# One product of 512 columns for the high and low parts of a gathered chunk, and a window sum folded by VectorE

## The reference

```python
def _mean_aggregate(x, src, dst, n_nodes):
    msg = x[src]                                              # gather 100,000 rows
    summed = jax.ops.segment_sum(msg, dst, num_segments=n_nodes)
    deg = jax.ops.segment_sum(ones, dst, num_segments=n_nodes)
    return summed / jnp.maximum(deg, 1.0)[:, None]

def _sage_conv(x, src, dst, Wl, bl, Wr, n_nodes):
    return _mean_aggregate(x, src, dst, n_nodes) @ Wl.T + bl + x @ Wr.T

# layer 0: messages weighted by relation and gate, summed over dst, updated, + x, layernorm
x = _layernorm(x + _L0_gnn_ref(x, ...))
# layers 1 to 3: three convolutions, relu behind the first two; then + x, layernorm
h = relu(_sage_conv(x, ..., W1l, b1l, W1r))
h = relu(_sage_conv(h, ..., W2l, b2l, W2r))
x = _layernorm(x + _sage_conv(h, ..., W2l, b2l, W2r))
```

## Time and profile before

| | us |
|---|---|
| median of 3 runs | 3801.09 |
| lowest and highest | 3783.49 and 3802.06 |
| the profiled execution | 3782.04 |
| its span, first to last instruction | 3779.7 |
| PE busy | 3080.2 (81%) |
| DVE busy | 2509.8 (66%) |
| ACT busy | 2338.1 (62%) |
| POOL busy | 2150.0 (57%) |

### The profile page before, as it was taken

One profiled execution on the slowest core, in us unless ns is written; L12 is line 12 of the kernel. 1 busy time (PEld: TensorE's weight loads), 2 busy tenths in 40 slices (PEclk: granted clock), 3 DMA queues, 4 the chain that ended last, 5 costly groups with the idle time before them and its releaser, 6 DMA issues. The chain is left out here.

```text
span 3779.7 us, 55957 instructions
## 1 busy us (share of the span) xinstructions
PE 3080.2 (81%) x17027; PEld 2611.1 (69%) x17027; DVE 2509.8 (66%) x5700; ACT 2338.1 (62%) x4157; POOL 2150.0 (57%) x1993
## 2 busy tenths in 40 slices
PE   5468887887878778777759999949999986999985
PEld 4356666666666666666648888847888865777774
DVE  8857777777777777777736565635555654666676
ACT  1066666666666666666548787728777845777761
POOL 5266666666666666666436555555555555555551
PEclk6589999999998998899979999979999988999998
DMA  4245555555454554455456565455555537555552
GB/s 124 82 128 146 136 138 146 139 135 143 132 141 131 141 136 133 132 140 135 118 188 199 171 192 183 149 175 183 175 178 168 179 107 229 189 175 187 177 155 80
DMA packets 345442, 575.72 MB, mean 152 GB/s; under 512 B 44709, under 2 KB 242678, under 8 KB 345142
## 3 DMA queue, kind: packets, MB, share of 16 engines
q1 hardware_dynamic: 249753, 316.82, 27.2%
q0 software_dynamic: 91872, 252.80, 24.1%
q10 hardware_dynamic: 3517, 2.48, 0.2%
HBM read 487.13 MB, written 84.78 MB: 151 GB/s over the span
## 5 line engine op out<-in xcount | busy, mean ns | idle before, releaser
L1484 POOL DMA_INDIRECT rows_arena<-table_h,src_idx x936 | 989.6, 1057 | 858.4 <-DVE row_pairs L1825 515.9
L1484 POOL DMA_INDIRECT rows_arena<-table_scaled_x,src_idx x782 | 889.4, 1137 | 574.4 <-DVEq L1759 333.4
L2053 PE MATMUL bank<-wide_counts,h_pairs 128*128 128x512 f32 (+1 forms) x4704 | 1085.9, 386 | 155.1 <-ACT wide_counts L1633 125.7
L2053 PEld LDWEIGHTS bank<-wide_counts,h_pairs 128*128 128x128 f32 x4704 | 854.5, 194 | 329.5 <-issue 143.1
L1990 PE MATMUL bank<-rel_pairs,ftype_hot 125*128 125x258 f32 x4688 | 758.0, 312 | 53.0 <-issue 53.0
L1833 DVE TENSOR_TENSOR h_pairs<-rows_arena,h_pairs 128x512 fp32r<-128x512 f32 x600 | 399.5, 681 | 528.7 <-ACT h_pairs L1630 394.4
L1990 PEld LDWEIGHTS bank<-rel_pairs,ftype_hot 125*128 125x128 f32 x4688 | 666.7, 204 | 87.6 <-issue 58.7
L1633 ACT CAST wide_counts<-rows_arena 128x1024 fp32r<-128x1024 bf16 (+1 forms) x600 | 634.7, 1058 | 74.4 <-DMA rows_arena<-edge_counts 74.1
L1630 ACT CAST h_pairs<-rows_arena 128x512 fp32r<-128x512 f32 x600 | 367.7, 613 | 354.8 <-PE bank L2053 213.6
L1654 ACT CAST rows_arena<-bank 128x448 bf16<-128x448 f32 (+1 forms) x940 | 426.4, 505 | 259.1 <-remote 98.8
L2039 PE MATMUL bank<-rows_arena 128*128 128x448 bf16 (+1 forms) x940 | 262.5, 363 | 323.1 <-ACT rows_arena L1654 227.1
(11 more groups left out here) (186 smaller groups left out, 3265.5 us busy)
## 6 DMA issues: line engine op xcount, KB each, us to landing
rows_arena<-edge_counts SPq DMA_DIRECT2D x273, 512.0 KB
edge_counts<-fcount SPq DMA_DIRECT2D x60, 832.0 KB
rows_arena<-in_edge_type_dram SPq DMA_DIRECT2D x195, 187.5 KB
rows_arena<-table_h SPq DMA_DIRECT2D x36, 512.0 KB, 12.1
rows_arena<-table_h,src_idx POOLq DMA_INDIRECT x936
rows_arena<-table_scaled_x,src_idx POOLq DMA_INDIRECT x782
table_h<-chunk_info SPq DMA_DIRECT2D x96, 128.0 KB
rows_arena<-edge_counts SPq DMA_DIRECT2D x39, 256.0 KB
```

The costliest lines, as they stand in the source:

```text
L1484: pool.indirect_dma_start(out=rows[:, g % ring, c, :], out_offset=None, in_=table[:, :], in_offset=bass.IndirectOffsetOnAxis(ap=src_idx[:, ...
L2053: last = pe.matmul(bank[2 + h][:, 0:cols_of(w)], h_pairs[:, v % HALVES, part, b % HALF, h * P:(h + 1) * P], wide_counts[:, v % HALVES, b % ...
```

## The change

The two products of a chunk become one: the moving operand is `row_pairs[slot, :, chunk, :]`, both parts, 512 columns, so the bank holds the sum of the high parts in its first 256 columns and that of the low parts in the other 256. `evacuate` on ACT now copies the second half of the bank to a new tile `window_lo` (one slot for all windows), after a wait for the fold of the window before. A new function on DVE, `fold_window`, adds `window_lo` to the first half of the bank and writes `window_sum`; it signals `s_evac` in ACT's place. It stands in DVE's stream right behind `row_lows(s + 1)`. Layer 0 keeps its code.

```diff
+                    window_lo = sb(f"window_lo{k}", [P, D], F32, tmp)
@@ evacuate, ACT
                                 act.wait_ge(s_seg, last_quad(w) + 1)
+                                if not first:
+                                    if w >= 1:
+                                        act.wait_ge(s_evac, w)
+                                    act.copy(window_lo[:, :], seg_bank[w % 2][:, D:2 * D]).then_inc(s_evac_lo, 1)
+                                    continue
@@ DVE
+                        def fold_window(slot):
+
+                            for w in [w for w in range(windows) if last_quad(w) + 1 == slot]:
+                                dve.wait_ge(s_evac_lo, w + 1)
+                                if w >= 2:
+                                    dve.wait_ge(s_turned, w - 1)
+                                dve.tensor_tensor(window_sum[:, w % 2, 0:D], seg_bank[w % 2][:, 0:D],
+                                                  window_lo[:, :], ALU.add).then_inc(s_evac, 1)
@@ DVE's slot
                                 if s + 1 < groups:
                                     row_lows(s + 1)
+                                fold_window(s)
@@ sums, PE
-                                    for part in range(2):
-                                        last = pe.matmul(seg_bank[w % 2][:, 0:sum_cols], hot[:, g % HOTS, c, :],
-                                                         row_pairs[:, g % ROW_PAIRS, part, c, :],
-                                                         start=(g % GW == 0 and c == 0 and part == 0),
-                                                         stop=(g == last_quad(w) and c == n - 1 and part == 1))
+                                    last = pe.matmul(seg_bank[w % 2][:, 0:2 * D], hot[:, g % HOTS, c, :],
+                                                     row_pairs[:, g % ROW_PAIRS, :, c, :], start=(g % GW == 0 and c == 0),
+                                                     stop=(g == last_quad(w) and c == n - 1))
```

More of the change, by code:

```diff
@@ L1431, in one_round_layer @@
                     s_hT, s_hT_cp, s_z = (lsem(n) for n in ("s_hT", "s_hTcp", "s_z"))
-                    s_row_hi, s_row_lo = lsem("s_row_hi"), lsem("s_row_lo")
+                    s_row_hi, s_row_lo, s_evac_lo = lsem("s_row_hi"), lsem("s_row_lo"), lsem("s_evac_lo")
+                    window_lo = sb(f"window_lo{k}", [P, D], F32, tmp)
                     s_half_hi, s_half_lo, s_wide, s_tile_read, s_half_used, s_dense_added = (
```

## The result

The changed kernel takes 3821.45 us (median of 7 runs, 3811.53 to 3832.67), the kernel before beside it 3801.09 us (7 runs, 3783.49 to 3809.03). The ratio is 1.0058, with an interval of 1.0030 to 1.0085: slower, by 20 us between the medians, and above the predicted range. The profiled execution took 3831.02 us (span 3829.2 us, granted clock 0.905), 49 us more than the one of before.

The account below looks back on a forecast made before the run. PE was taken to bound the steady parts, some 94% busy. Product -5.5 us and fold +2 gave -3.5 us; against the median of 3801.09 that is 3797.5, forecast as 3797 us, range 3768 to 3818.

Parts of the forecast that it names:

- The product, -5.5 us: PE's sums: four 512-column products replace eight of 256, 0.03 us less per group, 7.0 us over 234 groups, 80% gained.
- rival 1: PE's sums behind transposes: a real bubble disappears, 0.12 us per group, -20 to -26 us in all; 14% if it shows.
- The fold, +2 us: DVE's 78 added additions delay some low parts of gathered groups that PE awaits: 0 to 4.4 us, taken as 2.
- Rival 2: DVE's queue before the dense low parts: PE waits 0.47 us in each of 78 slots, +31 us, 3832; chance 10%.
- Its sign of 20 us or more in PE's waits for dense low parts: In the changed profile, PE's waits for dense low parts: under 4 us forecast, 20 or more would mean Rival 2.
- ACT's copy and the ends of layers, 0: ACT's copy adds no wait; the last window's longer way costs 0 to 0.6 us per layer, taken as 0.
- The median's level: Whole run: the median of runs lies 19 us above the profiled execution; about 0.5%, 19 us, can't be told from no change.
- 10 for the clock: PE's stretches at the lower clock: two or three more or fewer move the time 10 us either way, widening the range.

Follow-up runs that it names:

- the comparisons without late signals: Later series where no PE signal reached ACT late, kernel before near 3508 us; the changed kernel against it gave 0.9993, 0.9991 and 0.9989.
- the fold alone: Kernel before, products still 256 columns, plus a DVE maximum of bank and ACT's equal copy at the fold's place: 1.0113 with late signals, 1.0014 without.
- the first comparison: Against the kernel before (3740.29 us): only the fold added 1.0113, only 512-column products 0.9963, changed kernel with fold behind dense low parts 1.0002, unchanged 0.9990.
- the third: Against the kernel before (3508.28 us): changed kernel 0.9993, only the fold added 1.0014, only 512-column products 0.9974, changed kernel with fold one slot later 0.9994.

## Why the prediction was wrong

Against 3797 us forecast stand 3821.45. Against the comparisons without late signals the forecast change of -3.5 us stands well: -2.5, -2.5 and -3.1 us by the medians. That is luck in part, since both terms were too small and their errors cancel. The terms one by one:

- **The product, -5.5 us.** Sign right, size too small by the ratios: -9 us without late signals (0.9974, -6.4 by the medians) and -14 with them (0.9963, interval -22 to -6, -7.5 by the medians). The part that I could work out from distances, 7 us at full size, was itself too large: 512 columns out of two pieces cost 0.01 to 0.02 us less per group, not 0.03. That the bubble of rival 1 is bookkeeping was right.
- **The fold, +2 us.** This is the step that failed. Without late signals it is +5 (1.0014), a plain underestimate. With them it is +42 (1.0113, interval 28 to 56). The prediction bounded it with PE's waits for low parts of gathered groups, 0 to 4.4 us. Those waits did not grow. It dismissed the low parts of the dense halves because PE waited only 1.9 us for them; but that row counts PE's products alone. PE's weight loads wait for the same halves, 28.5 us in 16 waits in the kernel before, a row that I did not read. The slack at the dense halves was already gone there, 16 times in three layers. PE's products stood for 22 us of those waits; in the changed kernel the loads waited 49.6 us and the products stood for 43 of them. That is the size of the 21 us by which the layers grew. Nor had the sum a term for the clock: of the 48.2 us that the fold alone adds to the layers where signals are late, 22.8 are PE's busy time at a lower granted clock.
- **Rival 2, 10%.** It named the right place (the low parts of the dense halves) and nearly the right time, 3832 us. Its mechanism was wrong: not 0.47 us in each of 78 slots, but a few standstills of 3 to 6 us in a layer, where a burst of late signals finds the stock of halves short. Its sign of 20 us or more in PE's waits for dense low parts stands at 9.4 us by the row of the products and at 49.6 by that of the loads. -14 and +42 make +28; measured were +20, in another comparison and with parts that are loose by some 7 us.
- **ACT's copy and the ends of layers, 0.** Right: the copy waits 2.3 us in 2 waits, the fold never for the copy, and in layer 2 the last turn starts 5.48 us behind the last copy (5.17 before):

```profile
3141.97 1.16 PE L2028 MATMUL bank<-row_pairs,rel_pairs 128*128 128x512 f32 x4 [2.19 <-DVE row_pairs L1840]
3143.18 0.35 ACT L1647 COPY window_lo<-bank 128x256 f32<-128x256 f32 x1
3144.09 0.42 DVE L1834 TENSOR_TENSOR dst_f<-bank,window_lo 128x256 f32<-128x256 f32 x1
3148.66 0.38 PE L2040 MATMUL bank<-ident,dst_f 128*128 128x128 f32 x2
```

- **The median's level.** I took it as noise of 19 us, with 10 for the clock. In fact 233 us and more lie between comparisons of one and the same kernel (3740 and 3507 us), and the sign of this change goes with them.

Open is what makes PE's signals late. The DMA's own rows differ in one thing between the two kinds of execution. First the fold alone in the first comparison, then in the third (KB each, median us to landing):

```profile
rows_arena<-edge_counts SPq DMA_DIRECT2D x273, 512.0 KB
```

```profile
rows_arena<-edge_counts SPq DMA_DIRECT2D x273, 512.0 KB, 3.8
```

Both have the same 345443 packets, but in the first the profile could not tell when most transfers landed: many of its records of signals are missing, where the second has them. Late signals and missing records come together in all traces here. The Trainium skill, "NOTIFIC — the notification-queue block", Overflow: three behaviours, one of which stalls the engine, says that the block which writes such records can hold an engine up when its internal queues are full, rather than lose a record there. The holding up would fit the late signals, the missing records would not fit a block that loses none; no run here took the recording away, so nothing of it is shown. The late signals are not bound to a chip: comparisons with and without them ran on a chip of the same number.

## What to carry to other kernels

Before an operation goes in ahead of the producer of the busiest engine's operands, read that engine's waits by its weight loads as well as by its products, and find out whether the stock ahead of it ever runs out; a mean of idle time does not tell. Put what nobody is waiting for behind the work that somebody waits for: the same fold behind the dense halves cost a third as much. And where a profile of one core shows waits for "remote", take more than one comparison, at different times, before a verdict of half a per cent is believed.

## What was not expected of the hardware

- A signal of PE can reach ACT several microseconds after the modelled end of the products that send it: 6.3 and 8.2 us at the two places shown. In the first comparison that cost ACT 7.21 us at one place; in the third nothing. DVE waits for such signals too (76.6 us in 41 waits in layer 0 of the kernel before).
- The kernel before, one and the same program, took 3801, 3740 and 3507 to 3509 us in different comparisons. Most of that lies ahead of layer 1: the span is 3759.9 us in its profiled execution of the first comparison and 3510.7 in the fold alone of the third, and 210 of these 249 us lie there (layer 1 starts at 1908.5 and at 1698.8 us), over code that is the same in both.
- 512 moving columns out of two pieces 1024 elements apart stream no slower than eight products of 256, but save only 0.01 to 0.02 us of 0.94. The Trainium skill, "TensorE: Matmul & The Clock Gate", Back-to-back issue gap, gives N/2.4 + 2.5 ns between isolated products of N columns; the estimate from it is a saving of 10 ns to a group. The trace agrees with that size between dense blocks, 0.93 against 0.94 us.
